# Linear-attention feature map in one VectorE operation, memory weights on GpSimd, and turns written out in line

## What is computed

```python
x = x + attn_a(_layernorm(x))   # linear attention with memories
x = x + ffn(_layernorm(x))      # ternary weights, relu
x = x + attn_b(_layernorm(x))   # causal softmax attention with rotary positions
x = x + ffn(_layernorm(x))
```

```python
q, k, v = proj(w_q), proj(w_k), proj(w_v)
sq, sk = elu(q) + 1, elu(k) + 1                     # the feature map
out_m = einsum('bhsd,mhde->mbhse', sq, memories)
rel = einsum('bhsd,mhd->mbhs', sq, memory_norms)
out_m = out_m / clip(rel, EPS)
weights = softmax(rel.mean(axis=-1), axis=0)        # the memory weights, over the 4 memories
mem_out = einsum('mbhse,mbh->bhse', out_m, weights)
local = causal linear attention of sq, sk, v
out = g * mem_out + (1 - g) * local                 # g = sigmoid(gate), per head
return out @ w_o.T
```

## Time and profile before

| | |
|---|---|
| runs | 2298.64 us median of 3 (2289.67 to 2300.01) |
| the profiled execution's own time | 2286.95 us |
| its span, first to last instruction | 2285.2 us |
| mean granted clock of TensorE | 0.937 of full |
| busy shares of the span | PE 82%, PEld 53%, DVE 68%, ACT 60%, POOL 51% |
| first tiles of lane 1 alone | about 101 us |

### The profile page before, as it was taken

The page is one execution under the profiler, slowest core; times in us unless marked ns, Lnnn a source line. Parts: engine busy times, 40 slices in busy tenths (PEclk is TensorE's granted clock), DMA queues, the critical chain, the costliest instruction groups (busy, mean ns, idle before and its releaser), DMA issues.

```text
span 2285.2 us, 52784 instructions
## 1 busy us (share of the span) xinstructions
PE 1875.6 (82%) x18306; PEld 1217.1 (53%) x18306; DVE 1555.1 (68%) x3707; ACT 1366.5 (60%) x2694; POOL 1174.0 (51%) x1168
## 2 busy tenths in 40 slices
PE   0446788989889797989899797989889798988886
PEld 0223455656556565656555565656555555655543
DVE  5645676867677676867677676867677686876351
ACT  0215376766667575666667575756667565666644
POOL 0235447364665547364655647365665736464322
PEclk9857899999999899999999999989999999999988
DMA  3101211213031211203021211203021210302020
GB/s 105 55 10 56 66 57 47 64 32 95 30 80 53 66 66 48 57 30 103 30 74 58 67 66 31 74 30 103 30 66 66 66 49 29 94 29 66 10 57 10
DMA packets 79287, 127.10 MB, mean 56 GB/s; under 512 B 13616, under 2 KB 65968, under 8 KB 74928
## 3 DMA queue, kind: packets, MB, share of 16 engines
q1 hardware_dynamic: 70576, 115.07, 18.0%
q10 hardware_dynamic: 8448, 8.39, 1.1%
HBM read 80.95 MB, written 42.47 MB: 54 GB/s over the span
## 4 chain that ended last, share of the span: by engine, by line
issue 38%; POOL 33%; PE 14%; DVE 8%; DMA 2%; ACT 2%; SPq 1%; POOLq 1%; DVEq 0%; ACTq 0%
POOL place L650 9%; POOL place L660 7%; POOL place L667 3%; POOL place L710 3%; POOL place L688 3%; POOL rstd L632 2%; PE bank L1415 2%; DVE mxs L1270 2%; PE bank L1402 1%; PE bank L1581 1%; POOL xf L644 1%; PE bank L1554 1%; PE bank L1366 1%; POOL place L713 1%; DMA qst<-by_dim 1%
## 5 line engine op out<-in xcount | busy, mean ns | idle before, releaser
L1270 DVE TENSOR_REDUCE mxs<-bank 128x1 f32<-128x128 f32 (+3 forms) x1024 | 429.8, 480 | 107.5 <-PE bank L1556 107.4
L898 ACT ACTIVATE place<-bank 128x512 f32<-128x512 f32 (+1 forms) x768 | 349.6, 527 | 148.1 <-PE bank L1570 146.7
L660 POOL TENSOR_TENSOR place<-am,place 128x512 f16<-128x512 f32 x256 | 291.4, 1160 | 162.0 <-ACT place L804 162.0
L650 POOL TENSOR_TENSOR place<-place 128x512 f16<-128x512 f32 x256 | 307.5, 1210 | 85.3 <-ACT place L792 84.5
L1554 PE MATMUL bank<-kst,qst 96*128 96x128 f16 (+3 forms) x1024 | 242.1, 308 | 31.4 <-DMA qst<-by_dim 23.0
L1568 PE MATMUL bank<-qst,kst 128*128 128x512 f16 (+3 forms) x1024 | 236.8, 304 | 22.7 <-DMA qst<-nmt 11.9
L1415 PE MATMUL bank<-w2q,place 128*128 128x256 f16 x2048 | 249.9, 273 | 3.2 <-POOL place L650 1.6
L1415 PEld LDWEIGHTS bank<-w2q,place 128*128 128x128 f16 x2048 | 195.2, 98 | 41.4 <-issue 7.9
L1556 PE MATMUL bank<-mask_qk,identb 128*128 128x128 bf16 x1024 | 217.1, 223 | 0.0
L1094 DVE SCALAR_TENSOR_TENSOR am<-bank,tri 128x512 f32<-128x512 f32 x256 | 166.2, 686 | 73.9 <-PE bank L1433 59.0
L629 POOL TENSOR_TENSOR ve<-mv,epsc 128x4 f32<-128x4 f32 x64 | 13.0, 203 | 382.7 <-DVE mv L1040 382.7
(11 more groups left out here) (163 smaller groups left out, 4095.7 us busy)
## 6 DMA issues: line engine op xcount, KB each, us to landing
by_row<-place SPq DMA_DIRECT2D x128, 128.0 KB, 2.1
kst<-by_row SPq DMA_DIRECT2D x64, 256.0 KB, 3.3
qst<-by_row SPq DMA_DIRECT2D x32, 512.0 KB, 4.8
by_dim<-place SPq DMA_DIRECT2D x128, 128.0 KB, 3.1
kst<-by_dim SPq DMA_DIRECT2D x64, 256.0 KB, 3.9
qst<-by_dim SPq DMA_DIRECT2D x32, 512.0 KB, 6.2
xa<-x SPq DMA_DIRECT2D x16, 512.0 KB, 4.2
out<-xg ACTq DMA_DIRECT2D x16, 512.0 KB, 3.5
```

Of the source, the lines that this page charges most:

```text
L650: G.tensor_tensor(L.hl[:, m, :], L.hf[:, m % 2, :], L.hh[:, m, :], ALU.subtract).then_inc(s["hl"], 1)
L660: G.tensor_tensor(alp[:, n % 2, k, :], am[:, k, :], ahp[:, n % 2, k, :], ALU.subtract).then_inc(s["al"], 1)
L898: A.activation(pf[h % SLOTS][:, S2_COL[k]:S2_COL[k] + S2_W[k]], bank_of(L2, ("S2", h, k))[:, 0:S2_W[k]], ACT.Exp, scale=D ** -0.5 / RS ** ...
L1270: V.tensor_reduce(mxs[:, g:g + 1], bank_of(L2, ("S1", n, k))[:, Q_AT[i]:Q_AT[i] + (i + 1) * P], AX, ALU.max).then_inc(s["mx"], 1)
```

## The change

1. **The feature map.** elu(x)+1 is max(x, 0) + exp(-relu(-x)). ScalarE takes relu(-x) out of PSUM into ebuf and then, in place, the exponential of its negative; VectorE adds max(x, 0), straight from PSUM, in one operation. For this the Q and K weights are scaled by QS = 16 and not 128, and sq and sk carry a factor of 16, which other constants take out again. rbuf is gone, and the PSUM bank of a projection is free when sq is written.
2. **ssb** is written by ScalarE.
3. **Memory weights.** VectorE does one reciprocal, of wexp. GpSimd does the sum in two steps, the factor of the gate and the two products, all ahead of bsl. VectorE waits for them at the first `combine`.
4. **b2** is added in two operations of 128x512, and the feed-forward's result waits for each half.
5. **Turns in line.** The five `Fori` loops are Python loops, so turns 1 to 13 are written out.
6. MARKS has other numbers. TensorE and SyncE have the same instructions in the same order as before.

```diff
-AS = 2.0 ** -6
+QS = 16.0
+AS = 2.0 ** -8
...
-    jobs += [(("PA", t), "r", t + 1) for t in range(4)]
+    jobs += [(("PA", t), "sq", t + 1) for t in range(4)]
...
-            with sp.Fori(1, B - 2) as it:
+            for it in range(1, B - 2):
...
-                yield mark("XB")
-                pool.wait_ge(s["xn"], due(L, "xn", t, NT))
-                G.tensor_tensor(X[:, :, :], X[:, :, :],
-                                b2bc[:, :].rearrange("p (a f) -> p a f", a=1).broadcast_to([P, NT, H]),
-                                ALU.add).then_inc(s["xb"], 1)
+                for j in range(2):
+                    yield mark("XB", j)
+                    if j == 0:
+                        pool.wait_ge(s["xn"], due(L, "xn", t, NT))
+                    two = slice(2 * j, 2 * j + 2)
+                    G.tensor_tensor(X[:, two, :], X[:, two, :],
+                                    b2bc[:, :].rearrange("p (a f) -> p a f", a=1).broadcast_to([P, 2, H]),
+                                    ALU.add).then_inc(s["xb"], 1)
...
+            def memory_weights(t):
+
+                s = s1
+                pool.wait_ge(s["rexp"], due(L1, "rexp", t, 1))
+                G.tensor_tensor(wpair[:, :, :, :], wexp[:, :, 0:M // 2, :], wexp[:, :, M // 2:M, :],
+                                ALU.add).then_inc(s["rpair"], 1)
+                pool.wait_ge(s["rpair"], due(L1, "rpair", t, 1))
+                G.tensor_tensor(wsum[:, :].rearrange("p (a h) -> p a h", a=KH), wpair[:, :, 0, :], wpair[:, :, 1, :],
+                                ALU.add).then_inc(s["rsum"], 1)
+                pool.wait_ge(s["rsum"], due(L1, "rsum", t, 1))
+                G.tensor_tensor(wgate[:, :], wsum[:, :], gates[:, 0, :], ALU.mult).then_inc(s["rgate"], 1)
+                pool.wait_ge(s["rgate"], due(L1, "rgate", t, 1))
+                pool.wait_ge(s["rrec"], due(L1, "rrec", t, 1))
+                for r in range(2):
+                    heads = slice(r * QH, (r + 1) * QH)
+                    G.tensor_tensor(winv[:, :, r, 0:M, :], wrec[:, :, :, heads],
+                                    wgate[:, :].rearrange("p (a m h) -> p a m h", a=KH, m=1)[:, :, :, heads]
+                                    .broadcast_to([P, KH, M, QH]), ALU.mult).then_inc(s["rcoef"], 1)
...
-                    A.activation(ebuf[:, q % 2, :], bank_of(L1, ("PA", q))[:, :], ACT.Exp,
-                                 scale=1 / WS).then_inc(s["e"], 1)
+                    A.activation(ebuf[:, q % 2, :], bank_of(L1, ("PA", q))[:, :], ACT.Relu,
+                                 scale=-1 / QS).then_inc(s["below"], 1)
+                    act.wait_ge(s["below"], due(L1, "below", t, q + 1))
+                    A.activation(ebuf[:, q % 2, :], ebuf[:, q % 2, :], ACT.Exp, bias=small[:, 8:9],
+                                 scale=-1.0).then_inc(s["e"], 1)
...
+                yield at1("SS")
+                for half in range(KH):
+                    A.activation(ssb[:, half, :], onesf[:, :], ACT.Identity,
+                                 scale=ssum[:, half:half + 1]).then_inc(s["ssb"], 1)
...
-                    V.tensor_scalar(rbuf[:, q % 2, :], bank_of(L1, ("PA", q))[:, :], 1 / WS, 0.0,
-                                    ALU.mult, ALU.max).then_inc(s["r"], 1)
-                    dve.wait_ge(s["r"], due(L1, "r", t, q + 1))
-                    V.scalar_tensor_tensor(L1.sq[:, q, :], ebuf[:, q % 2, :], 1.0, rbuf[:, q % 2, :], ALU.min, ALU.add,
+                    V.scalar_tensor_tensor(L1.sq[:, q, :], bank_of(L1, ("PA", q))[:, :], 0.0, ebuf[:, q % 2, :],
+                                           ALU.max, ALU.add,
                                            accum_out=ssum[:, q // 2:q // 2 + 1] if q % 2 == 0 else None
                                            ).then_inc(s["sq"], 1)
...
-                yield at1("PA", 4)
-                dve.wait_ge(s["sq"], due(L1, "sq", t, 4))
-                for half in range(KH):
-                    V.tensor_scalar(ssb[:, half, :], onesf[:, :], ssum[:, half:half + 1], None,
-                                    ALU.mult).then_inc(s["ssb"], 1)
...
-                memory_weights_end(t)
+                yield at1("RE")
+                dve.wait_ge(s["rexp"], due(L1, "rexp", t, 1))
+                V.reciprocal(wrec[:, :, :, :], wexp[:, :, :, :]).then_inc(s["rrec"], 1)
```

More of the change, by code:

```diff
@@ L1 @@
+import math
 from contextlib import ExitStack
@@ L57 @@
 OUTS = dict(v=2, vh=2, sh=4, sl=4, bounced=128, wo=2, xres=2)
-FFN = dict(up=8, hf=8, hh=8, hl=8, xb=1, dn=2, xffn=2)
+FFN = dict(up=8, hf=8, hh=8, hl=8, xb=2, dn=2, xffn=2)
 PER1 = dict(
-    NORM, **OUTS, xin=16, proj=4, e=4, r=4, sq=4, sk=3, skt=3,
-    ssb=2, rm=1, rmax=1, rdif=1, rexp=1, rsum=1, rrec=1, rcoef=3,
+    NORM, **OUTS, xin=16, proj=4, below=4, e=4, sq=4, sk=3, skt=3,
+    ssb=2, rm=1, rmax=1, rdif=1, rexp=1, rpair=1, rsum=1, rgate=1, rrec=1, rcoef=2,
     st=2, bf=2, bh=2, bl=2, a=16, am=16, ah=16, al=16,
@@ L138 @@
             "T": [3.3],
[L139 to L146, removed]
+            "TT": [6.6],
+            "PB": [10.9, 12.6, 15.8, 18.1],
+            "PH": [15.3, 17.6, 21.1, 23.7],
+            "V": [25.4, 28.5],
+            "NM": [37.6, 56.8, 69.7, 82.9],
+            "NS": [43.2, 51.7, 53.7, 57.9, 60.2, 65.3, 67.7, 71, 75.6, 79, 81.6, 83.1, 87.9, 92, 93.5, 94.8],
+            "EV": [63.9, 77, 89.7, 99.6],
+            "OT": [104.7, 105.2],
         },
@@ L149 @@
             "T": [0],
[L150 to L157, removed]
+            "TT": [8.1],
+            "PB": [12.9, 13.7, 16.9, 19.2, 26],
+            "PL": [0, 16.1, 18.4, 24.8],
+            "N": [28.6, 30.2, 33.6, 35.2, 36.8, 40.4, 49.9, 52.6, 55.9, 59, 63.5, 66.9, 69.2, 71.9, 77.6, 80.6],
+            "NM": [37.9, 57.1, 70, 83.4],
+            "TP": [66.3, 80, 92.9, 102.6],
+            "OT": [105.4, 106.4],
+            "WO": [108.6, 114.2],
         },
         "pe": {
[L160 to L169, removed]
+            "TT": [4.9],
+            "PB": [9.4, 11.1, 13.3, 14.9],
+            "V": [16.2, 19.7],
+            "N": [28.1, 29.7, 32.2, 34.3, 35.9, 39.9, 44, 52, 55.2, 58.5, 63, 66.3, 68.6, 71.4, 76.9, 79.8],
+            "NM": [36.9, 56, 69.4, 82.3],
+            "NS": [41.9, 51.3, 53.2, 57.4, 59.7, 64.9, 67.3, 70.6, 73.5, 78.5, 81.2, 82.4, 86.1, 91.5, 93, 94.3],
+            "PV": [60.8, 74.7, 87.3, 97.1],
+            "TP": [65.6, 79.3, 92.3, 102],
+            "OT": [103.6, 104],
+            "WO": [107.1, 109.4],
         },
@@ L185 @@
             "FT": [2.9],
-            "FTT": [16.7],
-            "DN": [48.5, 55.7],
+            "FTT": [14.3],
+            "DN": [44, 51.5],
         },
         "pe": {
[L190 to L193, removed]
+            "FTT": [12.4],
+            "UP": [17.5, 18.9, 24.9, 26.7, 28.9, 30.5, 31.3, 33],
+            "DN": [33.1, 47.8],
+            "DM": [33.8, 34, 35, 35.2, 35.4, 35.7, 36.7, 37.9],
         },
@@ L728, in _ @@
             in_order(after(lane1_end(1), lane1_start(2)), lane2(0), lane_f1(1))
-            with pool.Fori(1, B - 2) as it:
+            for it in range(1, B - 2):
                 in_order(after(lane1_end(it + 1), lane1_start(it + 2)), lane2(it), after(lane_f2(it - 1), lane_f1(it + 1)))
@@ L929, in _ @@
             in_order(after(lane1_end(1), lane1_start(2)), lane2(0), lane_f1(1))
-            with act.Fori(1, B - 2) as it:
+            for it in range(1, B - 2):
                 in_order(after(lane1_end(it + 1), lane1_start(it + 2)), lane2(it), after(lane_f2(it - 1), lane_f1(it + 1)))
@@ L950, in _ @@
             link(V.memset(onesf[:, :], 1.0))
+            link(V.memset(small[:, 8:9], math.log(QS)))
             link(V.memset(L1.vp[:, :, :, :], 1 / AS))
@@ L993, in _ @@
             link(V.tensor_scalar(gates[:, 3, :], gates[:, 2, :], VS, None, ALU.mult))
+            link(V.reciprocal(gates[:, 0, :], gates[:, 3, :]))
             dve.wait_ge(pe_setup, 1)
@@ L1104, in combine @@
                         for r in range(2)]
+                if n == 0:
+                    dve.wait_ge(s["rcoef"], due(L1, "rcoef", t, 2))
                 for r in range(2):
                     dve.wait_ge(s["om"], due(L1, "om", t, 2 * n + r + 1))
-                    V.scalar_tensor_tensor(den[:, b, r, :, :], outs[r][:, :, :, D], MEM_EPS, winv[:, half, r, :, :],
+                    V.scalar_tensor_tensor(den[:, b, r, :, :], outs[r][:, :, :, D], QS * MEM_EPS, winv[:, half, r, :, :],
                                            ALU.max, ALU.mult).then_inc(s["clip"], 1)
@@ L1302, in _ @@
             in_order(after(lane1_end(1), lane1_start(2)), lane2(0), lane_f1(1))
-            with dve.Fori(1, B - 2) as it:
+            for it in range(1, B - 2):
                 in_order(after(lane1_end(it + 1), lane1_start(it + 2)), lane2(it), after(lane_f2(it - 1), lane_f1(it + 1)))
@@ L1653, in _ @@
             in_order(after(lane1_end(1), lane1_start(2)), lane2(0), lane_f1(1))
-            with pe.Fori(1, B - 2) as it:
+            for it in range(1, B - 2):
```

116 lines of the change are left out of this document (51 added, 65 removed), and 43 rows, old and new, of the table MARKS.

## The result

The changed kernel takes **2230.14 us**, median of 4 runs (2218.65 to 2237.34), against 2299.32 for the kernel before; the ratio is 0.9694, 95% interval 0.9635 to 0.9753. The forecast was 2205 with a range of 2165 to 2245: the direction and the range hold, and 25 us of the forecast gain did not come.

The account below looks back on a forecast made before the run. TensorE was busiest (82%); VectorE's gap at the loop's branch was put on the path, the memory weights as a second binding place. 2286.95 - 64.7 - 12.8 - 11.1 - 2 + 4 = 2200.4, +5: 2205 us, range 2165 to 2245.

Parts of the forecast that it names:

- Turns in line, -64.7: Loop's 12 turns, 128.5 us each less collisions, would take 123.1 like the one turn without a branch: 5.4 each.
- I take the value between: For turns in line, -64.7 was chosen between -41 (VectorE's two gaps only) and -83 (the clock's fall too).
- Rival 2: TensorE's clock stays up over turn boundaries (-18) and memory weights give all 1.88 us (-17): 2170; chance 0.20.
- Memory weights, -12.8 and -11.1: End of lane 1's start: fewer VectorE rows win 0.8 us in 16 turns; 5 long collisions with b2's addition go.
- the second idle time of the branch: VectorE's "issue" gap in front of L1094, 12 times, 7.9 us together, counted as cost of the branch back.
- Feature map, 0 with an upper end of +11: New map taken as 0; ends -6 (VectorE free earlier) and +11 (bank held longer, TensorE's third projection waits).
- 1.92 against 1.4 to 2.2: Latency in us for a quarter of the feature map, forecast for the new map against the old.
- -2 + 4: ssb on ScalarE saves 2 us at the kernel's start; fresh collisions cost 4; b2 in two pieces 0.
- The +4 for fresh collisions: Other VectorE rows may meet GpSimd's L652 once winv is written on GpSimd: +4 us, ends 0 and +12.
- Rival 1: Only the visible gaps at the branch go, 41 us, as TensorE binds behind them: 2229; chance 0.25.
- Rival 3: ScalarE's longer feature map or GpSimd's later bsl becomes the binding chain, eating 4 us a turn: 2269; chance 0.04.
- Rival 4: Slower, because engines wait to fetch the thirteen in-line copies of a turn: 2331; chance 0.02.

Follow-up runs that it names:

- e1: Kernel before with only turns 1 to 13 written in line: 2241.06 us, ratio 0.9734.
- e2: Changed kernel with the five loops put back, all else as in the change: 2261.46 us, ratio 0.9843.
- e11: Repeat of e8's kernel (changed kernel with old feature map and 14 added matmuls a turn), in the group of e9 and e12: 2209.2 us, ratio 0.9625.
- e12: Changed kernel with 14 added matmuls a turn that only keep TensorE busy: 2219.08 us, ratio 0.9664.
- e9: Changed kernel itself measured once more, in the group of e11 and e12: 2230.23 us, ratio 0.9709.
- e4: Changed kernel with the old memory weights back on VectorE, b2 still in two pieces: 2246.73 us, ratio 0.9768.
- e7: Changed kernel with both the old feature map and the old memory weights: 2243.69 us, ratio 0.9786.
- e3: Changed kernel with the old feature map, the change's scales kept: 2217.71 us, ratio 0.9646.
- e10: Kernel before, loops and old feature map kept, with only the memory weights moved to GpSimd: 2258.02 us, ratio 0.9834.
- e8: e3's kernel with 14 matmuls of 128x512 more per turn that only keep TensorE busy: 2208.34 us, ratio 0.9643.
- e5: e3's kernel with a projection's PSUM bank freed when sq is written, not after the cut at zero: 2237.8 us, ratio 0.977.
- e6: e3's kernel with one more ScalarE relu, into an unread tile, behind each exponential of the feature map: 2224.16 us, ratio 0.969.

## Why the prediction was right or wrong

- **Turns in line, -64.7 forecast.** Alone they give 58.6 (e1), from e2 on 31.3. The step that failed is "I take the value between, since it is a turn of this very program, measured". It was a single turn, and one in which TensorE's clock had hardly fallen (0.99). The 12 turns of e1, at 0.97, average 124.3 with the collisions taken off. Turns as short as the forecast's do come in the change, but only at that clock: 123.2 to 123.6 at 0.99, and 122.57, the forecast's 122.4, where the clock is held and the map is the old one (e11). The very turn that the forecast measured takes 125.35 in the change, at 0.97. There TensorE waits 1.94 us for the DMA of qst at 398.95 and comes out of it at the lower level; in the kernel before it waited 1.10 there, at 396.65, and stayed at the higher one. What makes the DMA land later is not shown.
- **The clock.** Rival 2 had the size of it nearly right: up to 1.2 us a turn, 18 in all. Measured with the added matmuls it is 11 (e12 against e9). So much is shown to be the clock's; the rest of the spread of the turns is not. It did not come by itself, because TensorE still idles there with no branch: 2.41 and 1.25 us, for VectorE's mask and low part.
- **Memory weights, -12.8 and -11.1.** 16.6 (e4) and 26 (e7 to e3) in line, 40 with loops (e10), so 24 lies between the two values for the kernel in line. The start of L1085 is as worked out. In the loop part of it is the second idle time of the branch, which I had counted under the branch. Two terms had one cause in common and could not be added; in the sum before to after each is counted once.
- **Feature map, 0 with an upper end of +11.** Measured +12 (e3) and +10 with the clock steady (e12 against e11); with the old memory weights +3 (e4 against e7), within the spread of such differences. The place is the bank, as the upper end said, but at the fourth projection. The step that failed is the comparison of latencies, 1.92 against 1.4 to 2.2, with TensorE's wait only at the upper end of the range: the bank was free after the cut at zero, one VectorE row before the end, and the end is what I compared. The time to the release is what counts: 0.61 + 0.72 + 0.69 and handovers now, behind the 0.45 for which ScalarE comes late.
- **The exponential, 0.63 taken, 0.72 measured.** Its bias is a column in SBUF. The Trainium skill (ScalarE: Activation LUTs, section What ACT_TABLE_LOAD costs) says that each such operand adds about 93 ns; the rows, 722 against 630, agree. The Trainium skill's rule on relu (the same page, section Rules for kernel authors), which the prediction set against its rows, finds no support in the trace after: the relu takes 594 ns on ScalarE, and the cut at zero took 687 on VectorE before.
- **ssb, b2: -2 + 4.** e7 against e1, +2.6 across two groups: no gain, and no more can be said. The +4 for fresh collisions was not priced alone.
- **Rivals.** Rival 1 gave 2229 and has the number in part by accident: it said that in line only the visible gaps come, 41 us. With the rest of the change in, that is near (31.3, where e2's list has 32.6); alone it is not (58.6 in e1). Rival 3 is wrong: L1286 does not wait for the map. Rival 4 is refuted: over the turns in line VectorE has 0.4 us of "issue" idle in two entries in the 12 turns, and TensorE 2.5 in twelve over the whole run, none over 0.3. The rule of the Trainium skill on taken branches (Runtime: NRT & Kernel Launch, section Instruction fetch mechanics) agrees with the rows on both sides, 2.7 us idle at the branch and next to none in straight code; that the idle time is a fetch stands on the page alone.

The missing 25 us can be followed along the chain before, e1, e7, e3, change. The forecast started from 2292 (2286.95 and the 5), 7 below the median of 2299.3. Turns in line gave 6 less than forecast, ssb and b2 cost 1 more, the memory weights gave 2 more, and the map cost 12: 7 + 6 + 1 - 2 + 12 = 24, and 25 but for the rounding. The sum must close, since the chain ends at the change; two of its steps join different groups and are uncertain by some 5 us each. That the range held is no proof of the sum: its largest single miss, the map, was a term put at 0. e8's version (all of the change but its feature map, and 14 matmuls more) beats both kernels, 2208.3 and 2209.2 us in two groups.

## What to carry to other kernels

When two edits act on the same stretch, price them in both orders. Here one idle time belonged to both the branch and the rows in the loop. Where an edit moves the last reader of a PSUM bank, compare times to the release of the bank, not to the end of the step. A single turn is not a mean; look at its granted clock before taking it as typical.

## What the runs showed that I had not expected

- Fourteen matmuls of 128x512 a turn, 3.4 us of TensorE's time put into its idle time, make the kernel 11 us faster (e12 against e9), though TensorE is the busiest engine.
- A branch back showed two idle times on VectorE, 2.7 and 0.66 us, and the second vanished when the memory weights, four rows of VectorE, left the loop (e10, e2).
- Freeing a bank one VectorE row later costs 20 us of 2218 (e5). A second activation that holds up no bank costs some 6, no more than the spread of the runs (e6).
